# A two-layer graph network on one core: more slots for gathered rows, a group's one-hots in one compare, and histogram one-hots in runs of 16

## The chip, the cores and the metric

One Trainium2 chip, one core of it. The metric is device time in microseconds (us) of one execution, the median over runs. Lower is better.

## The reference, cut to what matters

A graph of 6250 nodes with 128 features, 100,000 directed edges and a self loop on each node; the edges come sorted by destination.

```python
h = maximum(layernorm(x), 0)
for W_l, W_r, b in ((W_l0, W_r0, b0), (W_l1, W_r1, b1)):      # two layers
    agg = segment_sum(h[src], dst) / maximum(count(dst), 1)
    h = relu(agg @ W_l + h @ W_r + b)
x = x + h
h = maximum(layernorm(x), 0)
m = segment_sum(relu([h[src], h[dst]] @ W_interact + b_interact), src) / sqrt(16)
x = x + relu((h + m) @ W_update + b_update)
```

## The kernel before, in words

The program is written out for five engines, each with its own stream of instructions, joined by semaphores: PE (matrix products), DVE (vector), ACT (activations), POOL (GpSimd) and SP (DMA issue). Nothing is scheduled by a tool; the order on every engine is the order of the code.

**The stages.** After some preparation (layer norm, node numbers, counts) come the first layer, the second layer, and a message stage with the final update. `first_layer` and `second_layer` go over sixteen slabs of sixteen units each (`NS`, `SU`). A slab is a dense count matrix from all source nodes to 320 destination nodes. In the first layer DVE writes a unit's one-hots (`hot_unit`, lines 1759 and 1764), PE multiplies them into counts (`build`, line 1199), ACT copies the counts out of the accumulator into the slab (line 986), and PE multiplies the slab of before by the features (`dense_part`, line 1210); SP stores 14 of the slabs in device memory (3.9 MB each, line 653). The second layer loads them again and multiplies (line 1226).

**The tail.** The slabs end at node 5120. Edges to the nodes above come in 20 groups (`GD`) of 8 tiles (`KT`) of 128 edges. For each tile POOL gathers the 128 source rows by an indirect DMA (`fetch_tail`, line 858), DVE writes a 128 x 128 one-hot of the destinations (`tail_onehots`, line 1819), and PE multiplies rows by one-hots, 16 products a group (`tail_group`, line 1266). DVE then scales the sum (line 1828), PE multiplies it by the layer's weights (`tail_weigh`, line 1272), and DVE adds that to the result (line 1729). `TAIL_AT` spreads the groups over the units, in the first layer from slab 4 on, about eight units apart, in the second from slab 2 on, nine to ten apart. One-hots are placed 4 units ahead of the group's product, the sum's scaling 7 (second layer 3) units behind, the adding 4 units behind that.

**What orders the gathers.** They go in order through POOL's queue into a ring of slots, `tail_rows`, as many as `RT`: in the first layer laid over the tensors `tslot` and `rest`, in the second over `hot`. A gather into a used slot waits for the sum of the group that used it (semaphore `w_sum`), checked once for each eight:

```python
if i >= RT and (i == RT or (i - RT) % KT == 0):
    pool.wait_ge(w_sum, L * GD + (i - RT) // KT + 1)
```

PE's product of a group waits for its eight gathers (`e_gath`) and for its one-hots (`w_hot`). The one-hots have two buffers, so those of a group wait for the sum of the group two before.

**The sort.** Beside the first layer DVE also runs five stages a slab of a sort of the edges (`sort_stage`, lines 1864 and 1865), beside the second ten.

**The histogram.** In slab 1 the edges' source blocks are counted in four quarters of 208 columns (`HIST_AT`: after units 1, 5, 9 and 13). DVE writes 15 one-hots a quarter (`block_onehots`, line 1794), 7 of the high part of the number and 8 of the low part, and PE multiplies them two units later (`histogram`, line 1293). DVE's next quarter waits for that product. `spread_blocks` and `blocks_counted` add up the result in slab 2; POOL writes an index pattern for it beforehand (line 840).

Of the kernel before, what the change touches and what calls it, by code (L numbers as in the profile page):

```python
# [6 lines left out]
def gnn_kernel(nc, x, src, dst, W_l0, W_r0, b0, W_l1, W_r1, b1, W_int, b_int, W_upd, b_upd, out):  # L7
    f32 = mybir.dt.float32
    i32 = mybir.dt.int32
    f16 = mybir.dt.float16  # L10
    f32r = mybir.dt.float32r
    bf16 = mybir.dt.bfloat16
# [129 lines left out]
    KC = sum(n == DENSE for n in FROM)  # L142
    RT = 12
    assert all((k + 1) * PER + stray((k + 1) * PER) < n + P <= ROWS for k, n in zip(range(K0, NK), FROM))
# [47 lines left out]
    with ctx:  # L192
# [9 lines left out]
        def sem(name):  # L202
# [128 lines left out]
            tslot[:, :, :].rearrange("p s n -> p (s n)").bitcast(f16),  # L331
            rest[:, :, :].rearrange("p s n -> p (s n)").bitcast(f16)) for k in range(RT // 2)],
            [hot_b.bitcast(f16)[:, k * RB:(k + 1) * RB] for k in range(RT)]]
        hrow_f = hrow[:, :, :, :].rearrange("p s t f -> p (s t f)")
        tail_hot = hrow_f[:, 0:KT * P].bitcast(f16).rearrange("p (s t n) -> p s t n", s=2, t=KT)
        tail_sum = hrow_f[:, KT * P:KT * P + P]
        tail_dst = lnw[:, :, :].rearrange("p k t -> p (k t)")[:, 0:GD * KT]
        tail_inv = [cells[:, 0:ROWS - DENSE], work[:, 0:ROWS - DENSE]]
        assert RT * RB <= 2 * CAP and GD * KT <= 5 * NT and ROWS - DENSE <= min(KW, 2 * CW)

# [19 lines left out]
                  for k in range(2)]  # L360
        hist_hot = [keys[k][:, :].bitcast(bf16)[:, 0:QT * n].rearrange("p (t n) -> p t n", n=n)
                    for k, n in enumerate((HH, HL))]
# [379 lines left out]
        def _(pool):  # L742
# [78 lines left out]
            def link(instruction):  # L821
# [17 lines left out]
            pool.wait_ge(AS[0]["hot"], 1)  # L839
            p.iota(hist_at.rearrange("p (h t n) -> p h t n", h=HH, t=TH), pattern=[[1, HH], [HH, TH], [0, HL]], base=0,  # L840
                   channel_multiplier=-1, allow_small_or_imprecise_dtypes=True).then_inc(k_hl, 1)
# [7 lines left out]
            def fetch_tail(L):  # L849
                rows_stored(L)  # L850
                if L == 0:
                    pool.wait_ge(PS_[0]["own_ok"], NC)
                for i in range(GD * KT):
                    at = L * GD + i // KT
                    if i >= RT and (i == RT or (i - RT) % KT == 0):
                        pool.wait_ge(w_sum, L * GD + (i - RT) // KT + 1)
                    t = K0 * KT + i + 1
                    p.indirect_dma_start(tail_rows[L][i % RT], None, t_rows[L],  # L858
                                         bass.IndirectOffsetOnAxis(ap=pairs[:, t, 0:1], axis=0)
                                         ).then_inc(e_gath[at % 3], 16)  # L860
# [257 lines left out]
        def _(pe):  # L1118
# [135 lines left out]
            def tail_group(L, g):  # L1254
# [8 lines left out]
                for j in range(KT):  # L1263
                    rows = tail_rows[L][(g * KT + j) % RT]
                    for k in range(HALVES):
                        last = t.matmul(to, rows[:, k * P:(k + 1) * P], tail_hot[:, at % 2, j, :],  # L1266
                                        start=j == 0 and k == 0, stop=j == KT - 1 and k == HALVES - 1)
# [22 lines left out]
            def histogram(q):  # L1290
                pe.wait_ge(k_hist, 2 * q + 1)
                for k in range(0, QT, TH):
                    last = t.matmul(ps[0:TH * HH, 6, 0:TH * HL],
                                    hist_hot[0][:, k:k + TH, :].rearrange("p t n -> p (t n)"),
                                    hist_hot[1][:, k:k + TH, :].rearrange("p t n -> p (t n)"),
                                    start=q == 0 and k == 0, stop=q == HQ - 1 and k == QT - TH)
                last.then_inc(k_hist, 1)
# [180 lines left out]
        def _(dve):  # L1478
# [307 lines left out]
            def block_onehots(q):  # L1786
                if q == 0:
                    dve.wait_ge(k_hl, 1)
                else:
                    dve.wait_ge(k_hist, 2 * q)  # L1790
                part = slice(q * QT, (q + 1) * QT)
                for k, n in enumerate((HH, HL)):
                    for j in range(n):
                        last = v.tensor_scalar(hist_hot[k][:, :, j], blk_hl[k][:, part], float(j), None, ALU.is_equal)
                last.then_inc(k_hist, 1)
# [9 lines left out]
            def blocks_counted():  # L1805
                dve.wait_ge(s_once, ONCE_BLOCKS)
                for k, n in enumerate((4, HH - 4)):
                    link(v.tensor_reduce(
                        out=share[:, 4 * k * HL:(4 * k + n) * HL].rearrange("p (h n) -> p h n", h=n),
                        in_=ps[:, 6 + k, 0:n * TH * HL].rearrange("p (h t n) -> p h n t", h=n, t=TH),  # L1810
                        op=ALU.add, axis=AX.X))
                v.memset(share[:, NB:HH * HL], float(CAP)).then_inc(k_share, 1)

            def tail_onehots(L, g):
                at = L * GD + g
                if at > 1:
                    dve.wait_ge(w_sum, at - 1)
                for j in range(KT):
                    last = v.tensor_scalar(tail_hot[:, at % 2, j, :], iota_w[:, :],
                                           tail_dst[:, g * KT + j:g * KT + j + 1], None, ALU.is_equal)  # L1820
                last.then_inc(w_hot, 1)

# [393 lines left out]
```

## Time and profile before

| What | us |
|---|---|
| Median of 3 runs | 1738.58 |
| Lowest and highest | 1731.12, 1761.67 |
| The profiled execution | 1740.11 |
| Its span, first to last instruction | 1738.3 |
| PE busy in the span (share) | 1445.5 (83%) |
| DVE busy | 1450.4 (83%) |
| ACT busy | 1010.6 (58%) |
| POOL busy | 1047.7 (60%) |

Busy times are those of one execution. A busy PE is not a PE at its peak, because products are pipelined and their ends are modelled. The stages are where the limits differ, so the busy share of the whole run says little; it has to be read by stretches of time. In the rows further down, L858 is line 858 of the program before; an idle time stands with the instruction that came after it, and the arrow names what ended it.

### The profile page before, as it was taken

To read this page: it belongs to the slowest core of one execution; us is meant where nothing else is said; L and a number is where in the kernel's file an instruction comes from. 1 tells how busy PE (TensorE), PEld (TensorE's weight loads), DVE (VectorE), ACT (ScalarE), POOL (GpSimd) and SP (SyncE) were. 2 spreads that over 40 slices of the span, in tenths; PEclk is the share of its full clock that TensorE was granted. 3 is DMA by queue.
4 is the path that set the end of the run, shared out by engine and by line. 5 is a ranking of instruction groups with operands and counts; after the bars stand their busy time and mean duration, and the time that the engine had idled before them with its cause. 6 is when DMAs were issued, how large, how long until landed. Compare 5 with 4: busy or idle time off the path is not lost. (4 is left out here: it accounts for less than half of the span.)

```text
span 1738.3 us, 43512 instructions
## 1 busy us (share of the span) xinstructions
PE 1445.5 (83%) x16208; PEld 1235.5 (71%) x16208; DVE 1450.4 (83%) x4572; ACT 1010.6 (58%) x1990; POOL 1047.7 (60%) x1033
## 2 busy tenths in 40 slices
PE   1605787686866998999999659999999999999998
PEld 1303566465755775677767649999999999999997
DVE  7968898699867944887876759999999999999997
ACT  1715476576655853000000548888888778888886
POOL 4364205868677302577770267777777777777773
PEclk9855799899988999999999879999999999999999
DMA  3004434545433505898986124444444444444442
GB/s 108 1 1 134 176 152 166 190 138 203 149 126 127 207 24 169 287 290 289 290 273 213 37 68 118 124 118 112 118 118 111 119 119 119 119 120 117 123 111 60
DMA packets 125004, 245.17 MB, mean 141 GB/s; under 512 B 21784, under 2 KB 76201, under 8 KB 124794
## 3 DMA queue, kind: packets, MB, share of 16 engines
q1 hardware_dynamic: 95179, 184.46, 31.8%
q0 software_dynamic: 28032, 57.34, 13.4%
q8 instruction: 130, 2.13, 0.5%
q10 hardware_dynamic: 1584, 0.59, 0.1%
q14 instruction: 79, 0.65, 0.1%
HBM read 172.37 MB, written 73.14 MB: 141 GB/s over the span
## 5 line engine op out<-in xcount | busy, mean ns | idle before, releaser
L986 ACT ACTIVATE slab<-ps 128x980 f16<-128x980 f32 x256 | 321.0, 1275 | 199.6 <-PE ps L1199 193.3
L1426 PE MATMUL ps<-slab,room 125*128 125x128 bf16 x6762 | 435.5, 219 | 0.0
L1426 PEld LDWEIGHTS ps<-slab,room 125*128 125x128 bf16 x6762 | 393.1, 98 | 0.0
L898 POOL DMA_INDIRECT cells<-b_rows,work x319 | 306.0, 959 | 97.1 <-issue 88.4
L1098 ACT ACTIVATE lnw<-iota_w,keys 128x126 f32<-128x126 f32 x900 | 291.0, 389 | 1.6 <-POOL slab L889 1.6
L1417 PE MATMUL ps<-inv,hot 125*128 125x128 bf16 x2700 | 260.5, 221 | 3.7 <-DVE hot L2092 3.7
L1210 PE MATMUL ps<-slab,room 128*128 128x320 f16 x1568 | 258.8, 306 | 0.1
L1199 PE MATMUL ps<-hot 128*128 128x245 bf16 x1024 | 166.2, 289 | 72.5 <-DVE hot L1764 68.1
L1226 PE MATMUL ps<-slab,room 128*128 128x320 f16 x1568 | 225.0, 299 | 0.0
L858 POOL DMA_INDIRECT tslot<-t_rows,pairs x82 | 131.3, 1601 | 131.9 <-PE ps L1266 100.0
L858 POOL DMA_INDIRECT hot<-t_rows,pairs x160 | 164.9, 1031 | 64.4 <-issue 45.1
L1226 PEld LDWEIGHTS ps<-slab,room 128*128 128x128 f16 x1568 | 152.6, 98 | 58.3 <-issue 2.6
L1210 PEld LDWEIGHTS ps<-slab,room 128*128 128x128 f16 x1568 | 156.5, 100 | 51.0 <-issue 0.5
L1199 PEld LDWEIGHTS ps<-hot 128*128 128x128 bf16 x1024 | 109.4, 117 | 112.3 <-DVE hot L1764 82.5
L1417 PEld LDWEIGHTS ps<-inv,hot 125*128 125x128 bf16 x2700 | 167.0, 98 | 17.2 <-issue 3.9
L1764 DVE TENSOR_TENSOR hot<-iota_hi,cell_hi 128x984 bf16<-128x984 bf16 x256 | 169.1, 661 | 0.0
L2101 DVE TENSOR_SCALAR room<-keys,up_c 125x256 bf16<-125x256 f16 (+2 forms) x754 | 163.0, 295 | 0.0
L858 POOL DMA_INDIRECT rest<-t_rows,pairs x78 | 128.8, 1652 | 39.8 <-issue 22.2
L1864 DVE TENSOR_TENSOR keys<-keys 128x256 f32<-128x256 f32 (+1 forms) x212 | 111.1, 524 | 35.9 <-ACT keys L969 18.7
L898 POOL DMA_INDIRECT cell_hi<-b_rows,work x116 | 111.5, 961 | 35.4 <-issue 32.9
L898 POOL DMA_INDIRECT cell_lo<-b_rows,work x115 | 109.8, 955 | 35.1 <-issue 31.1
L2134 DVE SCALAR_TENSOR_TENSOR msg_slab<-ps,msg_slab 128x384 fp32r<-128x384 f32 x200 | 109.5, 548 | 16.9 <-ACT msg_slab L1112 15.7
(345 smaller groups left out, 2363.0 us busy)
## 6 DMA issues: line engine op xcount, KB each, us to landing
slabs_d<-slab SPq DMA_DIRECT2D x14, 3920.0 KB, 12.1
slab<-slabs_d SPq DMA_DIRECT2D x98, 560.0 KB, 5.1
hot<-lane_d SPq DMA_DIRECT2D x50, 576.0 KB
keys<-up_d SPq DMA_DIRECT2D x50, 128.0 KB
inv<-inv_row SPq DMA_DIRECT2D x32, 160.0 KB, 5.5
cells<-b_rows,work POOLq DMA_INDIRECT x319
keys<-down_d SPq DMA_DIRECT2D x50, 96.0 KB
t_rows<-room SPq DMA_DIRECT2D x1, 3200.0 KB, 13.7
```

The source lines that it names most:

```text
L858: p.indirect_dma_start(tail_rows[L][i % RT], None, t_rows[L], bass.IndirectOffsetOnAxis(ap=pairs[:, t, 0:1], axis=0)).then_inc(e_gath[at % ...
L898: p.indirect_dma_start(rows_g[gi % RS][:, j, :], None, b_rows, bass.IndirectOffsetOnAxis(ap=node_t[:, t:t + 1], axis=0)).then_inc(e_gath[g ...
L986: a.activation(slab[par][:, :, u * UB * BW:(u + 1) * UB * BW].rearrange("p h (k d) -> p k h d", k=UB), psum_unit(u).rearrange("p k (h d) - ...
L1098: last = a.activation(far[:, j, :], iota_w[:, 0:BE], ACT.Square, bias=lane_g[:, gi * GT + j:gi * GT + j + 1])
L1199: last = t.matmul(to[:, k, :], lo[:, :, k], hi[:, k, 0:HB], start=True, stop=True)
L1210: last = t.matmul(ps[:, 4 + s % 2, 0:SC], table[:, h, term, :], slab[s % 2][:, h, :], start=k == 0, stop=k == HI * HALVES - 1)
L1226: last = t.matmul(ps[:, 4 + q % 2, 0:SC], table[:, h, term, :], slab[q % 2][:, h, :], start=k == 0, stop=k == HI * HALVES - 1)
L1417: last = t.matmul(to, lanes_of, a_terms[0:BN, b % 2, k, :], start=k == 0, stop=not picked and k == TERMS - 1)
L1426: last = t.matmul(to, end_hot[g // 3][0:BN, u:u + P], bt[0:BN, bt_at(tile, w), k, :], start=False, stop=w == w1 - 1 and k == TERMS - 1)
L1764: v.tensor_tensor(out=hot[:, u % 4, P * UB:(P + HB + 1) * UB].rearrange("p (k w t) -> p k w t", k=UB, t=2), in0=iota_hi[:, :].rearrange("p ...
L1864: v.tensor_tensor(out=new[0], in0=old[0], in1=old[1], op=ALU.max if down else ALU.min)
L2101: last = v.tensor_scalar(end_hot[h][0:BN, at * P:(at + n) * P], row, numbers[0:BN, w:w + 1], None, ALU.is_equal)
```

## The change

There are three edits.

1. The ring of gather slots has 20 slots in the first layer and 18 in the second, instead of 12 in each. The waits for `w_sum` move accordingly.
2. The eight one-hots of a tail group are written by one `tensor_tensor` of 1024 columns. It compares a row of numbers (`iota_hi`) with each tile's destinations, which a new copy, made once, holds twice side by side in fp16 over the tensor `blk`.
3. The histogram's one-hots are laid out so that 16 columns of one number lie side by side; before, neighbouring columns lay 7 or 8 elements apart. The index pattern and the last reduction follow the new order.

```diff
-    RT = 12
+    RT = (20, 18)
...
+        tail_twice = blk[:, :].bitcast(f16)[:, 0:2 * GD * KT].rearrange("p (t e) -> p t e", e=2)
...
-        hist_hot = [keys[k][:, :].bitcast(bf16)[:, 0:QT * n].rearrange("p (t n) -> p t n", n=n)
+        hist_hot = [keys[k][:, :].bitcast(bf16)[:, 0:QT * n].rearrange("p (s n t) -> p s n t", n=n, t=TH)
...
-                    if i >= RT and (i == RT or (i - RT) % KT == 0):
-                        pool.wait_ge(w_sum, L * GD + (i - RT) // KT + 1)
+                    if i >= RT[L] and (i == RT[L] or (i - RT[L]) % KT == 0):
+                        pool.wait_ge(w_sum, L * GD + (i - RT[L]) // KT + 1)
...
-                for k in range(0, QT, TH):
+                for k in range(QT // TH):
                     last = t.matmul(ps[0:TH * HH, 6, 0:TH * HL],
-                                    hist_hot[0][:, k:k + TH, :].rearrange("p t n -> p (t n)"),
-                                    hist_hot[1][:, k:k + TH, :].rearrange("p t n -> p (t n)"),
+                                    hist_hot[0][:, k, :, :].rearrange("p n t -> p (n t)"),
+                                    hist_hot[1][:, k, :, :].rearrange("p n t -> p (n t)"),
...
                 for k, n in enumerate((HH, HL)):
+                    of = blk_hl[k][:, part].rearrange("p (s t) -> p s t", t=TH)
                     for j in range(n):
-                        last = v.tensor_scalar(hist_hot[k][:, :, j], blk_hl[k][:, part], float(j), None, ALU.is_equal)
+                        last = v.tensor_scalar(hist_hot[k][:, :, j, :], of, float(j), None, ALU.is_equal)
...
-                for j in range(KT):
-                    last = v.tensor_scalar(tail_hot[:, at % 2, j, :], iota_w[:, :],
-                                           tail_dst[:, g * KT + j:g * KT + j + 1], None, ALU.is_equal)
-                last.then_inc(w_hot, 1)
+                if at == 0:
+                    link(v.tensor_copy(tail_twice, tail_dst.unsqueeze(2).to_broadcast([P, GD * KT, 2])))
+                both = [P, KT, P // 2, 2]
+                v.tensor_tensor(out=tail_hot[:, at % 2, :, :].rearrange("p t (w e) -> p t w e", e=2),
+                                in0=iota_hi[:, 0:P].rearrange("p (w e) -> p w e", e=2).unsqueeze(1).to_broadcast(both),
+                                in1=tail_twice[:, g * KT:(g + 1) * KT, :].unsqueeze(2).to_broadcast(both),
+                                op=ALU.is_equal).then_inc(w_hot, 1)
```

POOL's order at the start of the first layer's gathers, before; `tslot` and `rest` are the slots, `w_sum` the sums of groups:

```order
283 L858 DMA tslot<-t_rows,pairs 128x256 [waits prep_own_ok_0,l_store0]
284 L858 DMA tslot<-t_rows,pairs 128x256 x5
285 L858 DMA rest<-t_rows,pairs 128x256 x6
286 L858 DMA tslot<-t_rows,pairs 128x256 [waits w_sum]
287 L858 DMA tslot<-t_rows,pairs 128x256 x5
288 L858 DMA rest<-t_rows,pairs 128x256 x2
289 L858 DMA rest<-t_rows,pairs 128x256 [waits w_sum]
```

Twelve gathers stand ahead of the first wait for a sum, and each further wait stands ahead of eight. The same place now:

```order
283 L859 DMA tslot<-t_rows,pairs 128x256 [waits prep_own_ok_0,l_store0]
284 L859 DMA tslot<-t_rows,pairs 128x256 x9
285 L859 DMA rest<-t_rows,pairs 128x256 x10
286 L859 DMA tslot<-t_rows,pairs 128x256 [waits w_sum]
287 L859 DMA tslot<-t_rows,pairs 128x256 x7
288 L859 DMA tslot<-t_rows,pairs 128x256 [waits w_sum]
```

Now twenty stand ahead of it; the count between waits is the same. On DVE, in slab 4, where the second group's one-hots stand between a unit's one-hots and a sort stage, before:

```order
500 L1759 TENSOR_TENSOR hot<-iota_lo,cell_lo 128x512 [waits agg_built_0]
501 L1764 TENSOR_TENSOR hot<-iota_hi,cell_hi 128x984
502 L1759 TENSOR_TENSOR hot<-iota_lo,cell_lo 128x512 [waits agg_built_0]
503 L1764 TENSOR_TENSOR hot<-iota_hi,cell_hi 128x984
504 L1819 TENSOR_SCALAR hrow<-iota_w,lnw 128x128 x8
505 L1775 TENSOR_TENSOR scaled<-ps,inv 128x320 [waits agg_added_0,agg_dense_0,s_inv0]
506 L1864 TENSOR_TENSOR keys<-keys 128x64x2x2 [waits q_step0,q_kept0]
```

and now:

```order
501 L1760 TENSOR_TENSOR hot<-iota_lo,cell_lo 128x512 [waits agg_built_0]
502 L1765 TENSOR_TENSOR hot<-iota_hi,cell_hi 128x984
503 L1760 TENSOR_TENSOR hot<-iota_lo,cell_lo 128x512 [waits agg_built_0]
504 L1765 TENSOR_TENSOR hot<-iota_hi,cell_hi 128x984
505 L1823 TENSOR_TENSOR hrow<-iota_hi,blk 128x1024
506 L1776 TENSOR_TENSOR scaled<-ps,inv 128x320 [waits agg_added_0,agg_dense_0,s_inv0]
507 L1869 TENSOR_TENSOR keys<-keys 128x64x2x2 [waits q_step0,q_kept0]
```

The eight tensor_scalars are one tensor_tensor, in the same place, with the same waits around it.

## Rows read from the trace of the kernel before

**Rows 1.** Busy us (instructions) of each engine by stretch; then PEclk, DMA share, GB/s.
```profile
core 0: us, PE busy (x) PEld busy (x) DVE busy (x) ACT busy (x) POOL busy (x), PEclk, DMA share, GB/s
160.00:208.00 48.00, 32.67 (x196) 22.25 (x197) 41.34 (x93) 22.48 (x18) 20.72 (x9) 0.71 0.46 159
...
297.90:325.10 27.20, 23.82 (x202) 18.71 (x201) 26.58 (x76) 20.30 (x17) 23.01 (x10) 1.00 0.48 176
325.10:366.00 40.90, 25.26 (x202) 19.76 (x200) 26.72 (x76) 20.31 (x17) 27.25 (x24) 0.87 0.39 139
...
265.50:585.50 320.00, 241.10 (x1944) 188.28 (x1943) 256.69 (x701) 195.63 (x156) 238.23 (x150) 0.93 0.47 164
690.00:945.00 255.00, 239.40 (x1940) 180.06 (x1938) 196.34 (x531) 21.27 (x29) 161.11 (x156) 1.00 0.86 276
```

**Rows 2.** Waits (total us, times, longest): PE, DVE 265.5 to 586; PE 690 to 945.
```profile
PE ps L1266 <- issue: 41.4, 5, 12.4
...
DVE hT L1729 <- PE ps L1272: 50.9, 14, 13.6
...
PE ps L1266 <- issue: 12.9, 13, 2.6
```

**Rows 3.** POOL's idle time ahead of line 858 (total us, times), 266 to 586; then 690 to 945.
```profile
  PE ps L1266: 117.6, 12
  issue: 41.4, 136
...
POOL hot L858 <- issue: 43.9, 144, 0.3
```

**Rows 4.** POOL's timeline (start, us), single gathers of the first layer.
```profile
266.87 3.05 POOL L858 DMA_INDIRECT tslot<-t_rows,pairs  x1 [83.71 <-PE ps L1266]
...
304.14 0.99 POOL L858 DMA_INDIRECT tslot<-t_rows,pairs  x1 [0.30 <-issue]
...
311.49 6.24 POOL L858 DMA_INDIRECT rest<-t_rows,pairs  x1 [0.30 <-issue]
...
331.30 0.94 POOL L858 DMA_INDIRECT tslot<-t_rows,pairs  x1 [0.30 <-issue]
```

**Rows 5.** Line 858 alone, by stretch: busy us (instructions), PEclk, DMA share, GB/s.
```profile
265.50:585.50 320.00, 235.61 (x148) 0.93 0.47 164
690.00:945.00 255.00, 161.11 (x156) 1.00 0.86 276
```

**Rows 6.** DVE's timeline beside those gathers.
```profile
304.23 1.65 DVE L1819 TENSOR_SCALAR hrow<-iota_w,lnw 128x128 f16<-128x128 f32 x8
...
316.25 0.66 DVE L1764 TENSOR_TENSOR hot<-iota_hi,cell_hi 128x984 bf16<-128x984 bf16 x1
317.46 0.35 DVE L1729 SCALAR_TENSOR_TENSOR hT<-ps,lift,hT 128x128 f32<-128x128 f32 x1 [0.55 <-PE ps L1272]
```

**Rows 7.** DVE's groups, 265.5 to 585.5: count | busy us, mean ns | idle before.
```profile
L1764 DVE TENSOR_TENSOR hot<-iota_hi,cell_hi 128x984 bf16<-128x984 bf16 x155 | 102.0, 658 | 0.0
...
L1819 DVE TENSOR_SCALAR hrow<-iota_w,lnw 128x128 f16<-128x128 f32 x152 | 31.7, 294 | 0.0
...
L1864 DVE TENSOR_TENSOR keys<-keys 128x512 f32<-128x512 f32 x7 | 4.8, 679 | 0.0
```

**Rows 8.** DVE's timeline: the histogram's first quarter and what follows it.
```profile
162.06 6.75 DVE L1794 TENSOR_SCALAR keys<-hrow 128x208 bf16<-128x208 bf16 x15
168.40 0.64 DVE L1759 TENSOR_TENSOR hot<-iota_lo,cell_lo 128x512 bf16<-128x512 bf16 x1
```

**Rows 9.** Groups of the whole run: tensor_scalars on two-byte types without strides.
```profile
L2101 DVE TENSOR_SCALAR room<-keys,up_c 125x256 bf16<-125x256 f16 (+2 forms) x754 | 163.0, 295 | 0.0
...
L2092 DVE TENSOR_SCALAR hot<-hot,up_c 125x384 bf16<-125x384 bf16 x300 | 76.7, 323 | 0.0
```

**Rows 10.** PE's timeline in the histogram's slab: seven products at either clock.
```profile
170.49 2.07 PE L1210 MATMUL ps<-slab,room 128*128 128x320 f16 x7
...
176.29 1.11 PE L1210 MATMUL ps<-slab,room 128*128 128x320 f16 x7
```

**Rows 11.** PE's products of the second layer's tail: ns, first and last start.
```profile
L1266 PE MATMUL ps<-hrow,hot x320: 216/219/219, 707.9 to 921.0; 128*128 128x128 f16 x160
```

More of the change, by code:

```diff
@@ L331, in gnn_kernel @@
             tslot[:, :, :].rearrange("p s n -> p (s n)").bitcast(f16),
-            rest[:, :, :].rearrange("p s n -> p (s n)").bitcast(f16)) for k in range(RT // 2)],
-            [hot_b.bitcast(f16)[:, k * RB:(k + 1) * RB] for k in range(RT)]]
+            rest[:, :, :].rearrange("p s n -> p (s n)").bitcast(f16)) for k in range(RT[0] // 2)],
+            [hot_b.bitcast(f16)[:, k * RB:(k + 1) * RB] for k in range(RT[1])]]
         hrow_f = hrow[:, :, :, :].rearrange("p s t f -> p (s t f)")
@@ L336, in gnn_kernel @@
         tail_sum = hrow_f[:, KT * P:KT * P + P]
+        tail_twice = blk[:, :].bitcast(f16)[:, 0:2 * GD * KT].rearrange("p (t e) -> p t e", e=2)
         tail_dst = lnw[:, :, :].rearrange("p k t -> p (k t)")[:, 0:GD * KT]
         tail_inv = [cells[:, 0:ROWS - DENSE], work[:, 0:ROWS - DENSE]]
-        assert RT * RB <= 2 * CAP and GD * KT <= 5 * NT and ROWS - DENSE <= min(KW, 2 * CW)
+        assert RT[0] * RB <= 8 * CW and RT[1] * RB <= 2 * CAP and 2 * max(RT) <= 5 * KT and GD * KT <= 5 * NT and ROWS - DENSE <= min(KW, 2 * CW)
         bt_all = slab[1][:, :, :].rearrange("p h n -> p (h n)").bitcast(bf16)
@@ L839, in _ @@
             pool.wait_ge(AS[0]["hot"], 1)
-            p.iota(hist_at.rearrange("p (h t n) -> p h t n", h=HH, t=TH), pattern=[[1, HH], [HH, TH], [0, HL]], base=0,
+            p.iota(hist_at.rearrange("p (h n t) -> p h n t", h=HH, t=TH), pattern=[[TH, HH], [0, HL], [1, TH]], base=0,
                    channel_multiplier=-1, allow_small_or_imprecise_dtypes=True).then_inc(k_hl, 1)
@@ L854, in fetch_tail @@
                     at = L * GD + i // KT
-                    if i >= RT and (i == RT or (i - RT) % KT == 0):
-                        pool.wait_ge(w_sum, L * GD + (i - RT) // KT + 1)
+                    if i >= RT[L] and (i == RT[L] or (i - RT[L]) % KT == 0):
+                        pool.wait_ge(w_sum, L * GD + (i - RT[L]) // KT + 1)
                     t = K0 * KT + i + 1
-                    p.indirect_dma_start(tail_rows[L][i % RT], None, t_rows[L],
+                    p.indirect_dma_start(tail_rows[L][i % RT[L]], None, t_rows[L],
                                          bass.IndirectOffsetOnAxis(ap=pairs[:, t, 0:1], axis=0)
@@ L1263, in tail_group @@
                 for j in range(KT):
-                    rows = tail_rows[L][(g * KT + j) % RT]
+                    rows = tail_rows[L][(g * KT + j) % RT[L]]
                     for k in range(HALVES):
@@ L1291, in histogram @@
                 pe.wait_ge(k_hist, 2 * q + 1)
-                for k in range(0, QT, TH):
+                for k in range(QT // TH):
                     last = t.matmul(ps[0:TH * HH, 6, 0:TH * HL],
-                                    hist_hot[0][:, k:k + TH, :].rearrange("p t n -> p (t n)"),
-                                    hist_hot[1][:, k:k + TH, :].rearrange("p t n -> p (t n)"),
-                                    start=q == 0 and k == 0, stop=q == HQ - 1 and k == QT - TH)
+                                    hist_hot[0][:, k, :, :].rearrange("p n t -> p (n t)"),
+                                    hist_hot[1][:, k, :, :].rearrange("p n t -> p (n t)"),
+                                    start=q == 0 and k == 0, stop=q == HQ - 1 and k == QT // TH - 1)
                 last.then_inc(k_hist, 1)
@@ L1809, in blocks_counted @@
                         out=share[:, 4 * k * HL:(4 * k + n) * HL].rearrange("p (h n) -> p h n", h=n),
-                        in_=ps[:, 6 + k, 0:n * TH * HL].rearrange("p (h t n) -> p h n t", h=n, t=TH),
+                        in_=ps[:, 6 + k, 0:n * TH * HL].rearrange("p (h n t) -> p h n t", h=n, t=TH),
                         op=ALU.add, axis=AX.X))
```

## The prediction

> **What bounds the kernel now.** I read the views in this order: the page's forty slices, to find where the tensor engine (PE) is not full; the busy times by stretch; the waits of PE and of the vector engine (DVE) in the stretches that the change touches; the gathers' own line on GpSimd (POOL); and two timelines.
>
> The message stage at the end, where the page's slices show a full PE, is not touched, so the change can act in three places. [Rows 1]: while the histogram is made (160 to 208) DVE is busy 41.3 of 48.0 us, and the granted clock averages 0.71, a mix of the two levels of 1.2 and 2.4 GHz. In the first layer one slab of sixteen units takes 27.2 us where it runs freely (297.9 to 325.1, DVE 26.58 busy), but 40.9 us in the next slab, where DVE is busy for the same 26.72. So DVE sets the pace there, and something else adds 14 us to some slabs. In the second layer (690 to 945) PE is busy 239.4 of 255 us and DVE only 196.3.
>
> [Rows 2] name what is added. PE stands 41.4 us in five waits ahead of the tail group's product (line 1266), and DVE stands 50.9 us for the tail's weighing product queued behind it on PE. "Issue" there means that no instruction released the wait: it is the landing of the gathered rows. In the second layer the same line waits 12.9 us in 13 pieces.
>
> **Why the rows come late.** With twelve slots the last four gathers of a group must wait for the sum of the group before. [Rows 3]: in the first layer POOL stood 117.6 us for line 1266, of which 83.7 were the first, harmless wait [rows 4], so 33.9 us in eleven. But POOL's own pace counts more. [Rows 3, 5]: 148 gathers took 235.6 us busy and 41.4 us between them, 277.0 us, 1.87 each, where a free one takes 0.94 + 0.30 = 1.25 (the gather at 331.30) [rows 4]. Others take up to 6.24 us [rows 4]. The gather at 311.49 ran while DVE did tensor_tensors only, and ended 0.8 us after DVE's last of them (316.25 + 0.66) left DVE idle until 317.46 [rows 6]; a free gather's 0.94 us, counted back from its end at 317.73, begins there too. The gather at 304.14, beside the old one-hots (L1819, tensor_scalar, 304.23 to 305.88), took 0.99. So gathers are held while DVE runs instructions with two SBUF inputs back to back.
>
> The Trainium skill (SBUF — State Buffer, "Who interferes with whom") says that a DVE instruction with two SBUF inputs contends with a GpSimd instruction that reads SBUF, the second to issue being blocked outright; it adds, as an inference, that tensor_tensor does not stall descriptor making. The trace agrees with the first and not with the second (6.24 us). By its first rule the change does harm: the tail's one-hots become a tensor_tensor with two SBUF inputs. That is the slower rival below.
>
> **First layer's tail, 265.5 to 585.5 (320 us).** *One-hots.* Eight tensor_scalars cost 31.7 us for 152, 0.209 each, 1.67 a group [rows 7]. The new one is an operation that the trace does not show in this size; the nearest is L1764, same engine, same paired pattern, 984 columns: 102.0/155 = 0.658, so 0.69 for 1024. Bounds: 0.66, as L1764 itself, and 1.36, twice the 0.679 of a 512-column tensor_tensor in fp32 [rows 7], if the mixed two-byte types are not packed; even that is no loss. I take 0.69, by the like pattern: 0.98 saved a group, 18.7 us over the 19 groups in this stretch. DVE's work falls from 256.7 to 238 us.
>
> *Slots.* Twenty gathers are there before the first group, so 140 remain. What does a gather cost while DVE is busy? DVE is idle for 320 − 256.7 = 63.3 us. If POOL's 33.9 us of slot waits all lay in that idle time, 29.4 us of it passed 23.5 gathers at 1.25 and the other 124.5 took 247.6 us, 1.99 each; if none did, 50.6 passed there and 97.4 took 213.7, 2.19 each. I take 2.1. Then 238 us of DVE work pass 113 gathers; the remaining 27 need 27 × 1.25 = 34 us in which DVE stands. 238 + 34 = 272, and 6 more for slot waits that stay and the landing of the last: 278 against 320, **−42 us**. So gathers, not DVE, set the end of this stretch: more slots take away the wait for a slot, and the pace of the gathers is late next. Best case, the gathers keep up entirely: 320 − 50.9 − 18.7 = 250, −70. Worst case, each costs 2.6 beside DVE because the one-hot windows are gone: 238/2.6 = 91, 49 × 1.25 = 61, 299, −21.
>
> **Histogram, four quarters of 15 one-hots.** The old run takes from 162.06 to the next instruction's start at 168.40, 6.34 us, 0.42 each for 208 columns [rows 8], written two bytes at a stride. The new ones write runs of 16. Unstrided two-byte tensor_scalars cost 163.0/754 = 0.216 (mostly 256 columns) and 76.7/300 = 0.256 (384) [rows 9]. I take 0.21; ends 0.18 (0.216 × 208/256) and 0.42 (no gain; a loss is excluded, since type and columns stay and only move closer together). 15 × 0.21 = 3.15, so 3.2 less a quarter, 12.8 in four, on an engine 86% busy there. PE's idle time shrinks with it and the clock may come up sooner: seven products took 2.07 us at 1.2 GHz and 1.11 at 2.4 [rows 10]. Against that, if PE stayed at 1.2 GHz it would take 2.07 + about 0.8 for the build, some 2.8 us a unit, 45 us for the slab, and only 3 us would be won. **−13 us**, between −3 and −17. The iota and reduction in the new column order move the same number of elements: nothing. The new copy of the node numbers is one small instruction with one wait, under 1 us: nothing.
>
> **Second layer.** PE sets the pace, so its 12.9 us come off whole if the gathers keep up. They cost (161.1 + 43.9)/156 = 1.31 [rows 3, 5], 10.5 us a group. Groups now come (921.0 − 1 − 707.9)/19 = 11.2 us apart [rows 11], and (212.1 − 12.9)/19 = 10.5 without the waits. So even, with 18 gathers in hand as a reserve. DVE's saving here is off the path (196 of 255 busy): nothing. **−12.5 us**; ends 0 and −15.
>
> **Sum.** −42 − 13 − 12.5 = −67.5. The profiled execution took 1740.1 (span 1738.3), so 1672.6; the median of the runs is 1.5 below it: **1671 us**.
>
> **Rivals.**
> 1. *The gathers stay starved* (the worst ends above): −21 − 5 − 4 = −30, 1709. For: POOL was the slow side in the free slabs too. Against: the one-hots' windows were only 32 of 257 busy us. 0.15.
> 2. *DVE alone sets the first layer*: −70 − 15 − 13 = −98, 1641. For: a held gather is chance, and 20 slots ride over one or two. Against: 2.1 us × 8 = 17 us a group, while DVE would ask for one each 12.5. 0.15.
> 3. *The change doesn't do what it says*: the rows land late because the slab store fills the DMA engines, and slots only queue the gathers earlier. The waits stay; the histogram's 13 and some 8 of the one-hots' 18.7 remain: 1718. Against: POOL's waits and long gathers explain the lateness alone. 0.04.
> 4. *Slower: lock-out by the new one-hots.* Let every group's one-hot hold POOL x us longer, in both layers. First layer: 20x us of POOL's time lost, 9.5x gathers, 11.9x us. Second: 142 × 1.31 + 20x against the 200 us that PE needs, so 20x − 14. It eats the 67.5 us at x = 2.6, one long gather in every other group; at x = 4 it is 67.5 − 48 − 66 = −46, hence 1785. For: the 6.24 us row. Against: the second layer's sort is tensor_tensors too, and its gathers still cost 1.31. 0.03.
>
> **How the numbers follow.** Forecast 0.63, within 1650 to 1700. The range of 1640 to 1708 reaches to the second rival and nearly to the first. A change of 2%, about 35 us, is what a measurement of this kernel tells from none: faster means under 1704. Faster: 0.60 of the forecast, all of the second rival, 0.05 of the first: 0.80. Slower: 0.03. Within: 0.17.
>
> **What would show it.** Right: the histogram's run takes about 3.2 us a quarter; line 1266's wait on PE falls from 41.4 to some 25 in the first layer and to under 3 in the second; POOL's wait for line 1266 is small after the first; gathers of 4 to 6 us are still there; the first layer's tail lasts about 278 us. Wrong: a one-hot over 1.2 us; gathers over 1.6 us on average in the second layer; or PE's waits in the first layer as long as before with POOL never waiting.

## The result and the profile after

The changed kernel takes 1645.62 us (median of 4 runs, 1644.32 to 1647.08), the kernel before, beside it on the same chip, 1749.78 (4 runs, 1731.12 to 1761.67). The ratio is 0.9486, 95% interval 0.9447 to 0.9524: faster by 5.1%. It leaves out two slow runs of before (1760.98 and 1761.67), so it is not the quotient of the two medians. The profiled execution took 1644.3, with a span of 1642.5 us; the span of before was 1738.3. So 95.8 us went, where 67.5 were forecast. The time is inside the range of 1640 to 1708 and the direction is right, but it lies below the 1650 to 1700 that the forecast gave itself, where the second rival stood (1641).

Busy time and share of the span after, by the page (before: PE 83%, DVE 83%):

```profile
PE 1429.2 (87%) x16208; PEld 1228.5 (75%) x16208; DVE 1394.0 (85%) x4293; ACT 1009.9 (61%) x1990; POOL 999.7 (61%) x1033
```

Both work a larger share of a shorter span; POOL's busy time fell by 48 us (from 1047.7), though it issues the same gathers. In the kernel after, the lines have moved: the gathers are L859, the tail's products L1267, the group's one-hots L1823, the histogram's one-hots L1796, the adding L1730.

**Where the 96 us went.** Engines by stretch after (busy us and instructions; then granted clock, DMA share, GB/s): slab 1 with the histogram, slab 2, two later slabs, and the two layers' tails from first to last product.

```profile
158.30:186.10 27.80, 26.30 (x200) 19.10 (x199) 25.14 (x93) 22.57 (x19) 23.23 (x16) 0.85 0.51 157
186.10:219.70 33.60, 26.07 (x187) 18.85 (x185) 23.99 (x50) 20.82 (x17) 6.93 (x2) 0.90 0.60 237
248.30:502.40 254.10, 230.87 (x1945) 182.62 (x1944) 238.17 (x568) 195.80 (x156) 181.12 (x142) 0.99 0.57 205
279.00:304.20 25.20, 23.55 (x203) 18.87 (x201) 24.66 (x62) 20.28 (x17) 19.41 (x14) 1.00 0.57 203
304.20:329.40 25.20, 23.52 (x202) 18.84 (x201) 24.66 (x61) 20.27 (x17) 20.32 (x17) 1.00 0.58 206
625.70:827.00 201.30, 195.94 (x1631) 149.97 (x1630) 147.56 (x323) 17.13 (x24) 147.98 (x143) 1.00 0.92 300
```

The columns after the stretch's length are PE, PE's weight loads, DVE, ACT, POOL. The first layer's tail took 320.0 us [rows 1] and takes 254.1: 66 less. DVE is busy for 238.2 of them, as forecast, and now sets the pace: 24.66 of 25.20 us in a slab, and no slab is like the one of 40.9 us in [rows 1]. The second layer's tail went from 213.3 (707.9 to the end of its last product) to 201.3: 12 less. The histogram's slab took 47.9 us and takes 27.8, but slab 2 went from 28.1 to 33.6. The first layer also began 2.0 us earlier, ahead of anything that the change touches. That is 20.1 − 5.5 + 66 + 12 + 2 = 95.

Slabs 1 and 2 before, in the same view:

```profile
160.30:208.20 47.90, 32.68 (x196) 22.16 (x195) 41.24 (x93) 22.20 (x19) 20.42 (x9) 0.71 0.46 158
208.20:236.30 28.10, 27.09 (x190) 19.90 (x189) 23.95 (x49) 21.14 (x17) 0.00 (x0) 0.91 0.38 150
```

Slab 1 shows what the shorter one-hots did: DVE 25.14 busy instead of 41.24, in as many instructions, at a granted clock of 0.85 instead of 0.71. In slab 2 DVE is as busy as before (23.99), so its 5.5 us more are waits.

PE's waits for the rows, after, in the second layer's tail (total us, times, longest); in the first layer's tail this line has none (before: 41.4 and 12.9, [rows 2]):

```profile
PE ps L1267 <- issue: 3.4, 3, 1.3
```

DVE's waits in the first layer's tail (before, the first was 50.9, [rows 2]):

```profile
DVE hT L1730 <- PE ps L1273: 8.7, 13, 1.9
```

The gathers alone, after: first layer from 248.3, second layer from 625.7 (busy us, instructions, granted clock, DMA share, GB/s); it answers to [rows 5].

```profile
248.30:502.40 254.10, 178.97 (x140) 0.99 0.57 205
...
625.70:827.00 201.30, 147.98 (x143) 1.00 0.92 300
```

A gather of the first layer was busy 235.61/148 = 1.59 us and is now 178.97/140 = 1.28. That is not shorter work but fewer held gathers: I counted those over 2 us in the timeline of the line, 24 of 148 before (107.8 us), 9 of 140 after (38.1 us). Some still are held, as POOL's timeline after shows (start, us; idle before):

```profile
249.65 3.66 POOL L859 DMA_INDIRECT tslot<-t_rows,pairs  x1 [56.32 <-PE ps L1267]
253.62 4.18 POOL L859 DMA_INDIRECT tslot<-t_rows,pairs  x1 [0.30 <-issue]
258.10 0.94 POOL L859 DMA_INDIRECT tslot<-t_rows,pairs  x1 [0.30 <-issue]
```

So the question for the experiments is why the gathers came in time in the first layer: because more slots ride over held gathers, or because fewer are held; and if fewer, what holds one.

### The profile page after: what moved, and what is told of

It is laid out like the page before. It is cut to its first block and busy times, and to the rows that moved or that the text cites. A ratio compares the mean times of both kernels' runs of the same rounds, so it can differ in the third digit from the quotient of the medians.

```text
span 1642.5 us, 43233 instructions
## 1 busy us (share of the span) xinstructions
PE 1429.2 (87%) x16208; PEld 1228.5 (75%) x16208; DVE 1394.0 (85%) x4293; ACT 1009.9 (61%) x1990; POOL 999.7 (61%) x1033
## 3 DMA queue, kind: packets, MB, share of 16 engines
q1 hardware_dynamic: 95179, 184.46, 33.6%
## 5 line engine op out<-in xcount | busy, mean ns | idle before, releaser
L1211 PE MATMUL ps<-slab,room 128*128 128x320 f16 x1568 | 252.2, 301 | 0.1
L1227 PE MATMUL ps<-slab,room 128*128 128x320 f16 x1568 | 225.0, 299 | 0.0
L1200 PE MATMUL ps<-hot 128*128 128x245 bf16 x1024 | 161.7, 283 | 49.3 <-DVE hot L1765 38.5
L859 POOL DMA_INDIRECT hot<-t_rows,pairs x160 | 165.7, 1036 | 51.7 <-issue 48.2
L859 POOL DMA_INDIRECT tslot<-t_rows,pairs x80 | 109.0, 1362 | 96.5 <-PE ps L1267 63.8
L2106 DVE TENSOR_SCALAR room<-keys,down_c 125x256 bf16<-125x256 f16 (+1 forms) x573 | 121.5, 291 | 0.0
```

The lines of the kernel that those rows point to most:

```text
L859: p.indirect_dma_start(tail_rows[L][i % RT[L]], None, t_rows[L], bass.IndirectOffsetOnAxis(ap=pairs[:, t, 0:1], axis=0)).then_inc(e_gath[a ...
L1200: last = t.matmul(to[:, k, :], lo[:, :, k], hi[:, k, 0:HB], start=True, stop=True)
L1211: last = t.matmul(ps[:, 4 + s % 2, 0:SC], table[:, h, term, :], slab[s % 2][:, h, :], start=k == 0, stop=k == HI * HALVES - 1)
L1227: last = t.matmul(ps[:, 4 + q % 2, 0:SC], table[:, h, term, :], slab[q % 2][:, h, :], start=k == 0, stop=k == HI * HALVES - 1)
L2106: last = v.tensor_scalar(end_hot[h][0:BN, at * P:(at + n) * P], row, numbers[0:BN, w:w + 1], None, ALU.is_equal)
```

## The experiments

All ratios are to the kernel before, run beside each kernel on its chip. "Held" means a gather of the first layer's tail, after those that fill the slots, that takes over 2 us (a free one takes 0.94).

**The three parts alone.** First the slots: the kernel before with

```diff
-    RT = 12
+    RT = (20, 18)
```

> The kernel before with the slots alone (20 and 18 instead of 12), old one-hots and old histogram. Three theories of why the rows came in time. Forecast's price (each gather costs 2.1 us beside busy DVE): 140 gathers against 257 us of DVE work give 257 + 18 x 1.25 + 6 = 285 us for the first layer's tail instead of 320, and the second layer gives 12: ratio 0.973. Reserve (20 slots ride over held gathers, and DVE sets the pace): about as many gathers over 2 us in the first layer's tail as before (24 of 148), yet PE's wait at line 1266 is under 5 us there; tail 257 + some 13 of other gaps = 270, second layer 12 less: ratio 0.964. Shape (it is the new one-hots that make held gathers rare, 9 in the changed kernel): 20 or more gathers over 2 us, PE still waits over 15 us, tail near 295: ratio 0.979.

Measured: 1701.67 us, ratio 0.9737 (0.9661 to 0.9813). The first layer's tail is 292.8 us, 25 gathers of 140 are held, and PE still waits:

```profile
PE ps L1266 <- issue: 15.7, 3, 8.8
```

Line 858 alone in that stretch, busy us and instructions:

```profile
263.70:556.50 292.80, 233.64 (x140) 0.96 0.50 178
```

A gather costs (233.64 + 140 × 0.30)/140 = 1.97 us on average. DVE is busy for 256.46 of the 292.8 us; if the 36.3 in which it stands pass 29 free gathers, the other 111 cost 2.16 each. So with the old one-hots the forecast's price of 2.1 beside busy DVE holds. The ratio is what that price gave; the tail, the number of held gathers and PE's wait are what was expected if the new one-hots make held gathers rare. The slots alone don't ride over the held gathers.

Then the one-hots alone, with 12 slots:

```diff
-                for j in range(KT):
-                    last = v.tensor_scalar(tail_hot[:, at % 2, j, :], iota_w[:, :],
...
+                v.tensor_tensor(out=tail_hot[:, at % 2, :, :].rearrange("p t (w e) -> p t w e", e=2),
```

> The kernel before with the one-compare one-hots alone, 12 slots, old histogram. Reserve and the forecast's price: the number of gathers over 2 us stays near 24, PE's waits at line 1266 stay near 41 us, and of DVE's 18.7 us only 5 to 10 come off: ratio 0.994 to 0.997. Shape: the gathers over 2 us fall to 10 or fewer with 12 slots too, PE's waits fall under 15 us, tail near 280: ratio 0.977. The rival of the forecast that these one-hots hold POOL: slower, over 1.0.

Measured: 1676.51 us, 0.962 (0.9554 to 0.9685). Only 7 gathers of 148 are held, the tail is 256.5 us, and the rows are almost never late. PE's waits for them in that stretch, then the gathers' line alone:

```profile
PE ps L1267 <- issue: 1.9, 2, 1.6
```

```profile
262.00:518.50 256.50, 181.77 (x148) 0.99 0.58 205
```

So in the first layer it is the one-hots that bring the rows in time, with 12 slots too. They save 18.7 us of DVE and take away most of PE's 41.4 us of waits.

And the histogram alone (with the index pattern and the reduction in the new order):

```diff
-                        last = v.tensor_scalar(hist_hot[k][:, :, j], blk_hl[k][:, part], float(j), None, ALU.is_equal)
+                        last = v.tensor_scalar(hist_hot[k][:, :, j, :], of, float(j), None, ALU.is_equal)
```

> The kernel before with the histogram's runs of 16 alone. If the three parts add up: slab 1 shorter by 20 us, slab 2 longer by 5.5 (PE waits for ACT, DVE for PE), so 14.6 less, the tail's 320 us as before: ratio 0.9915. If the phase between gathers and DVE decides how many are held, the tail may come out 10 us to either side at this shift of its start: 0.986 to 0.997.

Measured: 1724.82 us, 0.9885 (0.98 to 0.9969). Slab 1 takes 27.7 us, slab 2 32.7. The tail came out at 305.2 us with 25 held gathers, 15 less than before, and the second layer's at 223.5, 10 more: the tail varies by such amounts at the same number of held gathers, so this run agrees with the sum of 14.6 but does not prove it.

Alone the parts are worth 2.6, 3.8 and 1.2%, in sum 7.6; together they gave 5.1. Slots and one-hots cure the same waits: PE's 41.4 us in the first layer's tail fell to 15.7 with the slots alone and to 1.9 with the one-hots alone.

**One part taken back.** The changed kernel with 12 slots:

```diff
-    RT = (20, 18)
+    RT = (12, 12)
```

> The changed kernel with 12 slots in both layers again (one-compare one-hots and runs of 16 stay). If the one-hots alone bring the first layer's rows in time, the slots matter in the second layer only: first layer's tail 254 to 258 us with under 10 gathers over 2 us, PE's waits at line 1267 under 3 us there and 13 to 14 in the second layer (3.4 in the changed kernel), so 12 to 15 us more than the changed kernel: ratio 0.956. If the slots are needed in the first layer too (reserve), PE waits over 10 us there and the ratio is 0.965 or more.

Measured: 1662.56 us, 0.9554 (0.9514 to 0.9594). First layer's tail 259.3 us, PE waits 3.8 us in it, 9 held; second layer's tail 216.7, PE waits 14.5. Against the changed kernel that is 15.4 us more in the second layer's tail and 5.2 in the first's: the slots' worth is mostly in the second layer, as expected, but not all of it.

The changed kernel with the old one-hots:

```diff
-                v.tensor_tensor(out=tail_hot[:, at % 2, :, :].rearrange("p t (w e) -> p t w e", e=2),
...
+                for j in range(KT):
+                    last = v.tensor_scalar(tail_hot[:, at % 2, j, :], iota_w[:, :],
```

> The changed kernel with the eight tensor_scalar one-hots again (slots and runs of 16 stay). If these one-hots are what lets so many gathers be held: about 25 over 2 us again, PE waits some 15 us in the first layer, its tail 285 to 293 us instead of 254, second layer as in the changed kernel: ratio 0.968 to 0.973. If held gathers only need the reserve of 20 slots: tail 270 to 275, ratio 0.958 to 0.961.

Measured: 1679.44 us, 0.9632 (0.9573 to 0.9691). First layer's tail 285.6 us, 23 of 140 held, PE waits 8.9 us. The held gathers come back with the old one-hots, with 20 slots there. The ratio lies between the two expectations; the count and the tail say the first.

**What holds a gather.** In the kernel before, gathers ended about 0.9 us after DVE had stopped running tensor_tensors one behind the other [rows 4, 6]. If DVE's row of instructions holds them, a break in the row must free them, though it adds work:

```diff
                                 op=ALU.is_equal)
+                if s >= 4:
+                    v.memset(gap_t[:, u:u + 1], 0.0)
                 both = [P, UB, (HB + 1) // 2, 2]
```

> The kernel before, to which one memset of 1 column (no input) is added between the two one-hot instructions of every unit from slab 4 on: 192 instructions of some 0.06 us, 12 us of DVE work more. Lock-out theory (a gather is held until DVE runs an instruction that does not read two inputs from SBUF): such a one comes each 1.7 us now, so the gathers over 2 us fall from 24 to 5 or fewer, 148 gathers are busy some 185 us instead of 235.6, PE's waits at line 1266 fall from 41 to under 15 us, and the first layer's tail is 20 to 30 us shorter in spite of the added work: ratio about 0.985. Store theory (rows land late because the slab stores fill the DMA engines): gathers as long as before, waits as before, 12 us more work: ratio 1.003 to 1.007.

Measured: 1700.34 us, 0.9742 (0.9672 to 0.9811), with nothing else changed. No gather takes over 2 us (the longest 1.97), PE waits for no rows, and 148 gathers are busy for 159.59 us instead of 235.61. Line 859 alone, then a piece of POOL's timeline:

```profile
263.40:542.50 279.10, 159.59 (x148) 0.96 0.53 188
```

```profile
303.47 1.00 POOL L859 DMA_INDIRECT rest<-t_rows,pairs  x1 [0.30 <-issue]
304.78 1.07 POOL L859 DMA_INDIRECT rest<-t_rows,pairs  x1 [0.30 <-issue]
306.15 1.97 POOL L859 DMA_INDIRECT rest<-t_rows,pairs  x1 [0.30 <-issue]
308.42 1.21 POOL L859 DMA_INDIRECT rest<-t_rows,pairs  x1 [0.30 <-issue]
```

One column cleared in each unit made the kernel 2.6% faster. The slab stores are as before, so the store theory (third rival) falls.

The control puts an instruction with two SBUF inputs at the same place:

```diff
+                    v.tensor_tensor(out=gap_t[:, u:u + 1], in0=iota_w[:, 0:1], in1=iota_w[:, 1:2], op=ALU.add)
```

> The control to the added memset: at the same place in the kernel before, from slab 4 on, a tensor_tensor of 1 column that reads two inputs from SBUF. If what frees a held gather is an instruction that does not read two inputs from SBUF, this one frees none: 20 or more gathers over 2 us, some still over 5, PE's waits at line 1266 over 30 us, ratio 0.995 to 1.007. If any further start of an instruction (another phase) would do: under 5 gathers over 2 us, PE's waits under 5 us, ratio 0.975 as with the memset.

Measured: 1701.96 us, 0.9781 (0.9742 to 0.9819). It frees gathers too: 19 are over 2 us, but none over 3.15, and PE waits for none. My criterion (an instruction that does not read two inputs from SBUF) falls. POOL's and DVE's timelines of this kernel show when a gather is let go:

```profile
333.14 1.97 POOL L859 DMA_INDIRECT tslot<-t_rows,pairs  x1 [0.30 <-issue]
335.41 1.67 POOL L859 DMA_INDIRECT tslot<-t_rows,pairs  x1 [0.30 <-issue]
...
333.20 0.42 DVE L1867 TENSOR_TENSOR keys<-keys 128x256 f32<-128x256 f32 x1
333.53 0.41 DVE L1868 TENSOR_TENSOR keys<-keys 128x256 f32<-128x256 f32 x1
333.87 0.41 DVE L1760 TENSOR_TENSOR hot<-iota_lo,cell_lo 128x512 bf16<-128x512 bf16 x1
334.20 0.15 DVE L1765 TENSOR_TENSOR gap_t<-iota_w 128x1 f32<-128x1 f32 x1
...
336.18 0.14 DVE L1765 TENSOR_TENSOR gap_t<-iota_w 128x1 f32<-128x1 f32 x1
```

The first gather ends at 335.11; less a free gather's 0.94 that is 334.17, where the one-column instruction starts (334.20). It passed the starts of three larger ones (333.20, 333.53, 333.87) without being let go. The second, 337.08 − 0.94 = 336.14, falls to the next such start (336.18). Of 94 gathers in this tail that were late by 0.06 us or more, 58 were let go within 0.06 us of a start of line 1765. What lets go is thus a moment in which DVE reads little: an instruction of one column, of one SBUF input, or a pause. Whether type or size of the operands decides among the larger ones was not tried.

The kernel before agrees. None of its 24 held gathers is let go at the start of an instruction with both inputs in SBUF: 13 are let go within 0.06 us of the start of one that reads PSUM (the accumulator) and SBUF (lines 1729 and 1828), one at a tensor_scalar, and ten 0.10 to 0.13 us before the end of DVE's last instruction ahead of a pause. One of the 13, in POOL's and DVE's timelines of before (325.80 − 0.94 = 324.86):

```profile
320.76 5.04 POOL L858 DMA_INDIRECT rest<-t_rows,pairs  x1 [0.31 <-issue]
...
324.89 0.28 DVE L1828 TENSOR_TENSOR hrow<-ps,cells 128x128 f32<-128x128 f32 x1
```

So for the long holds the prediction's account, DVE's row of instructions with two SBUF inputs, stands in the kernel before; the one-column instruction is the exception to it.

**Why the new one-hots hold fewer.** The new instruction has two SBUF inputs itself, so it should not free anything. To see whether it is the length of DVE's row, the kernel with the new one-hots and 12 slots got idle work behind each group's one-hots in the first layer, reductions with one input whose results nothing uses:

```diff
+                for j in range(5 if L == 0 else 0):
+                    v.tensor_reduce(out=pad_t[:, at % 2, j:j + 1], in_=iota_w[:, :], op=ALU.add, axis=AX.X)
```

> The kernel before with the one-compare one-hots, and behind each of the first layer's groups five tensor_reduces of 128 columns to 1 (one input, some 0.2 us each, result unused), so that DVE's window for a group is about as long as with the old one-hots, 1.7 us. If the old one-hots' length or phase in DVE's row of instructions made gathers hit the wrong moment: 20 or more gathers over 2 us again, PE's waits over 15 us, tail 290 to 320, ratio 0.982 to 1.0. If it was their form (tensor_scalars), or the new one's: 10 or fewer over 2 us, PE's waits under 5, tail 256 + 19 = 275, ratio 0.973.

Measured: 1769.66 us, 1.0171 (1.0127 to 1.0215): slower than before. 36 of 148 gathers are held, the tail is 343.8 us, and PE waits 53.3 us. The waits of PE and of DVE in its tail (us in total, times, longest):

```profile
PE ps L1268 <- issue: 53.3, 8, 10.6
...
DVE hT L1731 <- PE ps L1274: 80.9, 13, 13.0
```

One held gather in POOL's timeline, the next one, and what DVE's timeline has beside them:

```profile
344.64 6.24 POOL L860 DMA_INDIRECT rest<-t_rows,pairs  x1 [0.30 <-issue]
351.19 0.94 POOL L860 DMA_INDIRECT rest<-t_rows,pairs  x1 [0.30 <-issue]
...
344.64 0.41 DVE L1872 TENSOR_TENSOR keys<-keys 128x256 f32<-128x256 f32 x1
...
349.40 0.66 DVE L1766 TENSOR_TENSOR hot<-iota_hi,cell_hi 128x984 bf16<-128x984 bf16 x1
360.64 0.35 DVE L1731 SCALAR_TENSOR_TENSOR hT<-ps,lift,hT 128x128 f32<-128x128 f32 x1 [10.58 <-PE ps L1274]
```

The gather starts together with one of DVE's instructions (344.64) and is let go (350.88 − 0.94 = 349.94) when DVE runs out of work, 0.12 us before the end of the one from 349.40. Then DVE stands 10.58 us for a product that is queued on PE behind one that waited 8.12 us for rows. DVE holds the gathers, and later waits for them. DVE is busy for 256.3 us here, as before (256.7), so it is not the work that makes this kernel slow.

With two reductions instead of five:

```diff
-                for j in range(5 if L == 0 else 0):
+                for j in range(2 if L == 0 else 0):
```

> The same kernel without the memset and with two reduces behind each group's one-hots instead of five. If more work of DVE in a group means more holds: between 7 and 36 gathers over 2 us, some 18, tail near 290, ratio 0.98. If it is where the starts of the gathers fall between the starts of DVE's instructions, the number need not lie between: under 7 or over 36 would show it, and it would not be told by this run if it lies between.

Measured: 1734.4 us, 1.002 (0.993 to 1.0111); 29 held, tail 314.8, PE waits 40.7 us. Between 7 and 36, so it does not tell amount of work from phase, as said beforehand. Most of the harm is there with two.

And the kernel with five reductions, with the memset in each unit as well:

```diff
+                if s >= 4:
+                    v.memset(gap_t[:, u:u + 1], 0.0)
```

> The kernel with one-compare one-hots and five reduces behind each (12 slots, 36 gathers over 2 us, tail 344 us), to which the memset of 1 column a unit from slab 4 on is added. If the holds make that kernel slow: the gathers over 2 us fall under 5, PE's waits from 53 us to under 5, the tail to 275 to 285 us, ratio 0.975. If the longer window itself, or the late one-hots, make it slow: tail 340 or more, ratio 1.01 to 1.03.

Measured: 1700.77 us, 0.988 (0.9709 to 1.005; the kernel before spread from 1710 to 1753 on this chip). 7 held, none over 2.29 us, no wait of PE for rows, and the tail 64 us shorter than without the memset:

```profile
263.40:543.30 279.90, 164.89 (x148) 0.96 0.54 188
```

So the held gathers were what made that kernel slow.

**A loss found beside the change.** In the changed kernel ACT, PE and DVE wait one for the other at slab 2's start. SP's issues there (start, us the queue was held, x1), then ACT's and DVE's rows:

```profile
139.58 9.77 SPq L628 DMA_DIRECT2D a_rows<-in_x  x1
149.41 32.37 SPq L639 DMA_DIRECT2D inv<-inv_row  x1
181.83 0.43 SPq L654 DMA_DIRECT2D slabs_d<-slab  x1
...
195.85 1.26 ACT L987 ACTIVATE slab<-ps 128x980 f16<-128x980 f32 x1 [7.54 <-DMA slabs_d<-slab]
...
201.12 1.28 DVE L1810 TENSOR_REDUCE share<-ps 128x32 f32<-128x512 f32 x2 [8.20 <-PE ps L1305]
```

The first slab's store is queued on SP behind a small load that is held for 32.37 us behind a copy of 3.1 MB, which only the message stage needs. In the kernel before, the store goes out as late (182.95), but slab 2 begins only at 208.2: the longer histogram hid it. So the copy was moved:

```diff
-            sp.dma_start(a_rows.rearrange("(t p) f -> p t f", p=BN), x.rearrange("(t p) f -> p t f", p=BN)
-                         ).then_inc(s_first, 16)
...
+                if s == STORED - 1:
+                    sp.dma_start(a_rows.rearrange("(t p) f -> p t f", p=BN), x.rearrange("(t p) f -> p t f", p=BN)
+                                 ).then_inc(s_first, 16)
```

> The changed kernel with one transfer moved: SP's copy of the input (line 628 there, 3.1 MB within device memory, needed in the message stage only) is issued after the last slab's store instead of ahead of the first slab. In the changed kernel the load behind it held SP's queue from 149.4 to 181.8, so the first slab was stored from 181.8 to 195.9, ACT waited 7.5 us for that, PE 6.0 for ACT and DVE 8.2 for PE, and slab 2 took 33.6 us instead of 28.1. If that is the chain: the store starts near 165, the three waits go, slab 2 takes 26 to 28 us, and the run is 5 to 8 us shorter than the changed kernel: ratio 0.944. If the store of the first slab then only collides with something else, or the copy does so at its new place: 0.947 to 0.951.

Beside it on the same chip, the changed kernel once more:

> The changed kernel itself, beside the one with the moved copy on the same chip: 1644 to 1647 us, ratio 0.945 to 0.952, and a profile with the same 9 or so gathers over 2 us in the first layer's tail.

Measured: 1636.9 us (6 runs, 1635.47 to 1640.93) against 1646.64 (6 runs, 1644.82 to 1651.13), 9.7 us less, where 5 to 8 were expected. By the ratio alone the second expectation would hold. But the ratios to the kernel before, 0.9504 (0.941 to 0.9598) and 0.9557 (0.9463 to 0.9652), are wide since that kernel ran from 1710 to 1753 on this chip; the two kernels' own runs don't overlap. With the copy moved, SP's first store in its timeline, then slabs 1 and 2 by stretch:

```profile
165.56 0.36 SPq L652 DMA_DIRECT2D slabs_d<-slab  x1
```

```profile
161.10:187.80 26.70, 25.22 (x200) 18.58 (x199) 25.02 (x93) 22.44 (x19) 22.43 (x15) 0.88 0.54 194
187.80:213.50 25.70, 24.17 (x187) 18.23 (x186) 23.97 (x49) 21.05 (x17) 6.95 (x2) 1.00 0.43 169
```

The store goes out at 165.56 instead of 181.83, and slab 2 takes 25.7 us instead of 33.6. This kernel beats both others. The changed kernel's second profile had 12 held gathers (9 in the first), and a tail of 258.2 us.

## Why the prediction was right or wrong

**What bounds the kernel: right for before, wrong for after.** DVE set the pace of the first layer's slabs, late rows added the rest, and the second layer's waits came off nearly whole. But after the change the gathers were to set the end of the first layer's tail, with some 25 us of PE's waits left. No such wait is left, and DVE sets it: busy for 238.2 of 254.1 us.

**The price of a gather beside busy DVE: the step that failed.** The prediction took 2.1 us and carried it over to the changed kernel. After, a gather costs (178.97 + 140 × 0.30)/140 = 1.58 on average, and 1.61 beside busy DVE if the 15.9 us in which DVE stands pass 12.7 free ones. Eight of them are 12.6 to 12.9 us, about the 12.5 in which DVE asks for a group, so the rows come in time. The price belongs to the row of instructions that DVE ran, not to busy DVE as such: with the old row it holds for 20 slots too (the run with the slots alone), with the new row the average is 1.5 with 12 slots ((181.77 + 148 × 0.30)/148). The prediction saw this coupling from the wrong side only: its worst end let the price rise to 2.6, because the one-hots' windows, in which gathers passed freely, would be gone; no end let it fall below 2.1 but the best case. "Gathers of 4 to 6 us are still there" was right (4.90 is the longest), but there are 9 over 2 us instead of 24. The first layer gave 66 us instead of 42; this is 24 of the 28 us by which the sum was short. That the time is still within the range is luck: the range reached down to 1640 for the second rival's sake, and that rival's reason was not the one at work.

**One-hots: right.** 0.69 us a group was forecast; DVE's group after, in the first layer's tail:

```profile
L1823 DVE TENSOR_TENSOR hrow<-iota_hi,blk 128x1024 f16<-128x1024 bf16 x19 | 13.1, 687 | 0.0
```

DVE's work fell to 238.2 us; forecast 238.

**Histogram: −13 forecast, −14.6 measured, with a gain of 5 and a loss of 5.5 that were not in its sum.** DVE's first quarter after, and what follows it:

```profile
160.05 2.60 DVE L1796 TENSOR_SCALAR keys<-hrow 128x208 bf16<-128x208 bf16 x15
162.56 0.41 DVE L1760 TENSOR_TENSOR hot<-iota_lo,cell_lo 128x512 bf16<-128x512 bf16 x1
```

2.51 us from start to start, instead of 6.34 before and 3.15 forecast: 0.167 an instruction, under the prediction's lowest, 0.18. Four quarters save 15.3; slab 1 gave 20.1, and the granted clock came up with it (0.85, against 0.71 before), which the prediction had named without a price. 5.5 were given back in slab 2, where the store was late (the run with the moved copy). The prediction had not asked what was next there; it should have, for SP's queue is in the same trace.

**Second layer: right.** −12.5 forecast, −12.0 measured, PE's waits from 12.9 to 3.4, so 2.5 of the 12.0 came from elsewhere. The run with 12 slots shows that this is the slots.

**Rivals.** The second (DVE alone sets the first layer, 1641) gave the right number for another reason: it said that 20 slots ride over held gathers, but with the new one-hots 12 do nearly as well (259.3 us against 254.1), and 20 don't with the old ones (285.6). The first (still starved) is out by the changed kernel itself, where PE waits for no rows in the first layer, and the third (stores fill the DMA engines) by the memset alone. The fourth let the new one-hots hold POOL because they read two inputs from SBUF. The rule it stood on (the Trainium skill, SBUF — State Buffer, "Who interferes with whom": such an instruction contends with GpSimd's reads) would have made the change do harm; here fewer gathers were held, 7 and 9 against 24. Yet a slower kernel was near: the same one-hots with 1.05 us of reductions behind them took 1.017 of the time of before.

**What stays open.** Why the old one-hots' eight instructions, or the new one with reductions behind it, let so many more gathers be held than the new one alone. In all these kernels a free gather comes every 1.25 us, and a unit's two one-hot instructions with one of the sort behind them take 0.335 + 0.58 + 0.335 = 1.25 of DVE from start to start as well, so that one gather's start can meet the same point of the row as the last one's. That would make the count a matter of phase. It fits, but no run shows it. The traces bear out a part. Take the gathers that start while DVE is in an instruction with two SBUF inputs and another such follows without a pause. In the kernel before, 30 of these start within 0.10 us of that instruction's start, and 19 are held; 39 start later in it, and 4 are held. In the changed kernel it is 5 of 21 and 4 of 91. So it matters where in an instruction a gather starts, and fewer start near its beginning after the change; but of those that do, fewer are held too, and that is not explained.

## What to carry to other kernels

A duration read beside another engine's work belongs to the order in which that engine runs it; if the change rewrites that order, the duration is to be bounded on both sides, below as well. Where gathers go out from POOL beside a DVE that runs large two-input instructions without a break, one tiny instruction among them can pay for itself (here 192 of 0.06 us made the first layer's tail 40.9 us shorter). And where a stage gets faster, look at every queue that feeds its end: what was hidden by the slow stage (here a small load held behind a copy on SP) comes due.

## What the runs showed that was not expected

- A memset of one column, 0.06 us, in each unit took away all 24 held gathers and gave 2.6% of the whole kernel. A tensor_tensor of one column did nearly the same.
- A gather that starts together with one of DVE's large instructions can be passed over at more than ten starts that follow (6.24 us; twelve more after the one at 344.64, up to the one at 349.40), while others are let go at such a start (31 of the 54 that took 1.00 to 2.00 us in the kernel before).
- A load of a 320-number row into all partitions held SP's queue for 32.37 us where a copy of 3.1 MB lay ahead of it; with the copy gone from there, the load ended its issue after 9.67 us and the store behind it went out 16 us sooner.
